# Softmax attention on one core: where a key tile's value matmuls stand in TensorE's order

## The chip, the core and the metric

One NeuronCore of a Trainium2 chip runs the whole program. Five engines work side by side, each through its own queue in order: TensorE (PE, whose weight loads are shown apart as PEld), VectorE (DVE), ScalarE (ACT), GpSimd (POOL) and SyncE (SP, which here only issues DMAs). They meet through semaphores. The metric is the device time of one execution in microseconds (us), the median of the runs. Lower is better.

## The reference, cut to what matters

The model is a chain of six blocks over 2048 tokens of 128 channels. The change touches the softmax attention alone:

```python
qkv = einsum('bsd,ed->bse', x, qkv_w) + qkv_b      # 16 heads of 8 channels
scores = einsum('bhqe,bhke->bhqk', q, k) / sqrt(8) # 2048 queries x 2048 keys for each head
attn = softmax(scores, axis=-1)
out = einsum('bhqk,bhke->bhqe', attn, v)
out = einsum('bsd,ed->bse', out, proj_w) + proj_b
```

The softmax needs the maximum of every query's row before it can take an exponential, so the kernel forms all scores twice: a first pass for the maxima, a second one for the exponentials.

## The kernel before

`softmax_attention` cuts the work into 16 **units**: 4 groups of 4 heads (`GROUPS`, `GH`) by 4 chunks of 512 queries (`CHUNKS`). Units are counted from 0. Units 4 to 11 (groups 1 and 2) run in a hardware loop over the group (L1336 for PE), the others are written out.

**First pass** (`first_pass`, L1253 to L1272): 64 matmuls in a unit, numbered i, each 128 queries by 512 keys, go through four PSUM banks, `S1B`. Two successive matmuls, i even and i+1, make a pair in two banks, and DVE reduces a pair to one column of maxima in one instruction (L1382). Only the even matmul of a pair waits, and it waits until the pair before the last one has been reduced (L1264 and L1265, quoted below). After the 32nd reduction DVE combines the maxima in seven short instructions (L1386 to L1403), and SP writes them into extra rows of `q` with four DMAs (L1175), on which the unit's second pass waits (L1307).

**Second pass** (`unit` of PE, L1288): it walks over 16 key tiles, kt = 0 to 15. For each tile and each of the four heads `score(s)` (L1300) makes one matmul of 128 keys by 512 queries into one of three banks, `S2B`, and waits until the exponential that last used the bank is done. ACT takes the exponential of each score, straight out of PSUM into the buffers `xT` and `xn` in turn (L1359). `weigh` (L1274 to L1286) multiplies the four heads' exponentials of one tile with the values `v`. It waits for all four exponentials of its tile, and is 4 matmuls in f32, which the trace shows as 8 short records, side by side on the array. It runs one tile behind: in tile kt, `weigh(kt - 1)`.

**How the two passes are woven.** While the second pass of a unit runs, the first pass of a later one is done in the gaps. `ahead(s)` (L1294) issues the first-pass matmuls of step s+`LEAD`, LEAD being 12, and the count for each step is in a table:

```python
done = [max(0, (k + 1 - HOLE) * STEPS // (STEPS - HOLE)) for k in range(-1, STEPS)]   # L1124
S1_IN = [range(done[k], done[k + 1]) for k in range(STEPS)]                           # L1125
# in first_pass, L1264 and L1265 (the condition cut): for an even i
pe.wait_ge(s1_used, (g * CHUNKS + qc) * PAIRS + (i // 2 - 1))
```

STEPS is 64 and HOLE is 3, so step k has no first-pass matmul for k = 0 to 2, one for most others, and two for k = 23, 43 and 63. Matmul i is that of step i+3 for steps 3 to 22, of step i+2 for steps 24 to 42, and of step i+1 for steps 44 to 62. Tile kt holds the steps k = 4kt+12 to 4kt+15, modulo 64. The last unit, 15, has nothing to do ahead, and unit 14 only in its tiles 0 to 12.

In what follows S0 to S3 are the four scores of a tile, A0 to A3 the first-pass matmuls that `ahead(s)` to `ahead(s + 3)` issue, W its `weigh`, and R a reduction of a pair on DVE (L1382). Before the change PE's order in a tile is S0 S1 A0 S2 A1 S3 A2 W A3 (L1308 to L1325).

Of the kernel before, what the change touches and what calls it, by code (L numbers as in the profile page):

```python
# [933 lines left out]
def softmax_attention(m):  # L934
# [32 lines left out]
    with ExitStack() as stack:  # L967
# [6 lines left out]
        @block.gpsimd  # L974
        def _(pool):
            for c in range(CHUNKS):
                norm.rstds(pool, c)

            step = Chain(pool, pool_steps)
            step(nc.gpsimd.memset(own_row[:, :], 0.0))  # L980
            for i in range(PARTS):
                step(nc.gpsimd.affine_select(out=own_row[:, :], in_=own_row[:, :], compare_op=ALU.not_equal, fill=1.0,
                                             base=-(ROWS + i * GH), pattern=[[-1, GH]], channel_multiplier=1))
            nc.gpsimd.memset(zeros[:, :], 0.0)
            nc.gpsimd.memset(neg_part[:, :, :], 0.0)
# [121 lines left out]
    with ExitStack() as stack:  # L1107
# [143 lines left out]
        @block.tensor  # L1251
        def _(pe):
            def first_pass(g, qc, i):  # L1253

                h, qt, kc = i // (TPC * CHUNKS), i // CHUNKS % TPC, i % CHUNKS

                if i == 0 and qc > 0:
                    pe.wait_ge(q_loaded[qc], DMAS_Q * (g + 1))
                elif i == 0 and not (isinstance(g, int) and g == 0):
                    pe.wait_ge(q_loaded[qc], DMAS_Q * g)  # L1260
                if qc == 0 and i % (TPC * CHUNKS) == 0 and not (isinstance(g, int) and g == 0):
                    pe.wait_ge(k1_loaded[h], DMAS_K * g)

                if i % 2 == 0 and not (isinstance(g, int) and g == 0 and qc == 0 and i < len(S1B)):  # L1264
                    pe.wait_ge(s1_used, (g * CHUNKS + qc) * PAIRS + (i // 2 - 1))  # L1265


                queries = q[0:ROWS, qc, h, :].rearrange("r (p t) -> r t p", t=TPC)[:, qt, :]
                mm = nc.tensor.matmul(m.ps[:, S1B[i % 4], :], queries,  # L1269
                                      k1[:, h, kc * CHUNK:(kc + 1) * CHUNK], start=True, stop=True)  # L1270
                if i % 2 == 1:
                    mm.then_inc(s1_ready, 1)  # L1272

            def weigh(g, qc, kt, first=False):  # L1274

                u = g * CHUNKS + qc
                if qc == 0 and kt % (TILES // 2) == 0:
                    pe.wait_ge(v_loaded[kt // (TILES // 2)], 16 * (g + 1))
                if kt == 0 and not first:
                    pe.wait_ge(out_stored, u)  # L1280
                pe.wait_ge(exped, u * STEPS + (kt + 1) * GH)
                for h in range(GH):
                    last = nc.tensor.matmul(m.ps[32 * h:32 * h + VC, AVB, :], v[:, kt, h, :],  # L1283
                                            ex[kt % P_RING][:, h, :], start=(kt == 0), stop=(kt == TILES - 1),
                                            skip_group_check=True)
                last.then_inc(av_done, 1)  # L1286

            def unit(g, qc, last, first=False):  # L1288

                u = g * CHUNKS + qc  # L1290
                after = [(g, qc + 1), (g, qc + 2)]
                after = [(a, b) if b < CHUNKS else (a + 1, b - CHUNKS) for a, b in after]

                def ahead(s):  # L1294
                    if last and (qc == CHUNKS - 1 or (qc == CHUNKS - 2 and s + LEAD >= STEPS)):
                        return
                    for i in S1_IN[(s + LEAD) % STEPS]:
                        first_pass(*after[(s + LEAD) // STEPS], i)

                def score(s):  # L1300
                    kt, h = s // GH, s % GH
                    if not (first and s < len(S2B)):
                        pe.wait_ge(exped, u * STEPS + (s - S2_SINCE[s] + 1))
                    nc.tensor.matmul(m.ps[:, S2_BANK[s], :], k2[:, h, kt * P:(kt + 1) * P], q[:, qc, h, :],  # L1304
                                     start=True, stop=True).then_inc(s2_ready, 1)

                pe.wait_ge(max_loaded, DMAS_M * (u + 1))  # L1307
                for kt in range(TILES):  # L1308
                    if qc == 0 and kt % (TILES // 2) == 0:
                        pe.wait_ge(k2_loaded[kt // (TILES // 2)], DMAS_K * (g + 1))  # L1310
                    s = kt * GH
                    score(s)
                    score(s + 1)
                    ahead(s)
                    score(s + 2)
                    ahead(s + 1)
                    score(s + 3)
                    ahead(s + 2)
                    if kt >= 1:
                        weigh(g, qc, kt - 1, first)  # L1320
                    elif qc >= 1:
                        weigh(g, qc - 1, TILES - 1)
                    elif not first:
                        weigh(g - 1, CHUNKS - 1, TILES - 1)
                    ahead(s + 3)  # L1325


            nc.tensor.matmul(m.ps[:, AVB, :], zeros[:, 0:P], zeros[:, :], start=True, stop=True)
            for i in range(STEPS):
                first_pass(0, 0, i)  # L1330
            for i in range(S1_IN[LEAD].start):
                first_pass(0, 1, i)
            unit(0, 0, False, True)
            for qc in range(1, CHUNKS):
                unit(0, qc, False)
            with pe.Fori(1, GROUPS - 1) as g:  # L1336
                for qc in range(CHUNKS):
                    unit(g, qc, False)
            for qc in range(CHUNKS):
                unit(GROUPS - 1, qc, True)  # L1340
            weigh(GROUPS - 1, CHUNKS - 1, TILES - 1)
# [72 lines left out]
    with ExitStack() as stack:  # L1414
# [3 lines left out]
        ahead = Prepare(m, stack, m.gateT, True, 5, 7)  # L1418
# [544 lines left out]
```

## Time and profile before

| what | value |
|---|---|
| median of 3 runs | 1883.54 us (1879.14 to 1883.91) |
| span of the profiled execution | 1880.9 us |
| PE busy over the span | 1635.9 us, 87% |
| DVE busy | 1354.7 us, 72% |
| ACT busy | 836.9 us, 44% |
| softmax attention, second pass | 264 to 1036 us of the span |

The profile shows one execution, and its span runs from the first to the last instruction. "Busy" is the time in which an engine executes, matmuls from start to written result, so that PE can look busy while its array waits. The timeline gives start and length of each instruction, or of a row of equal ones (x2, x4), then in brackets how long the engine had been idle and what it waited for. The start of a bf16 matmul of 512 columns to the start of the next one is 0.22 us at full clock, though each has a length of 0.38 us. The waits list says which line waited for which. The granted clock is given as a share of the full 2.4 GHz.

### The profile page before, as it was taken

To read this page: it belongs to the slowest core of one execution; us is meant where nothing else is said; L and a number is where in the kernel's file an instruction comes from. 1 tells how busy PE (TensorE), PEld (TensorE's weight loads), DVE (VectorE), ACT (ScalarE), POOL (GpSimd) and SP (SyncE) were. 2 spreads that over 40 slices of the span, in tenths; PEclk is the share of its full clock that TensorE was granted. 3 is DMA by queue.
4 is the path that set the end of the run, shared out by engine and by line. 5 is a ranking of instruction groups with operands and counts; after the bars stand their busy time and mean duration, and the time that the engine had idled before them with its cause. 6 is when DMAs were issued, how large, how long until landed. Compare 5 with 4: busy or idle time off the path is not lost. (4 is left out here: it accounts for less than half of the span.)

```text
span 1880.9 us, 23731 instructions
## 1 busy us (share of the span) xinstructions
PE 1635.9 (87%) x7285; PEld 683.8 (36%) x7285; DVE 1354.7 (72%) x1951; ACT 836.9 (44%) x1493; POOL 222.4 (12%) x145
## 2 busy tenths in 40 slices
PE   6987589999999999999998798899994356589999
PEld 3433112222222222222221443366661122256665
DVE  5776788888888778888880577666656999745654
ACT  2433427777676666667778253322223000042222
POOL 2222300000000000000000022211101324301110
PEclk8998659999999999999999899899996777799999
DMA  6000400011001100111000000000000000000000
GB/s 168 2 0 1 135 16 8 14 27 40 9 14 28 30 12 7 27 30 24 2 2 2 1 1 0 1 1 0 0 1 0 0 0 1 0 1 6 6 5 7
DMA packets 32021, 29.49 MB, mean 16 GB/s; under 512 B 7788, under 2 KB 27032, under 8 KB 31928
## 3 DMA queue, kind: packets, MB, share of 16 engines
q1 hardware_dynamic: 31928, 28.31, 5.9%
q8 instruction: 52, 0.85, 0.2%
q14 instruction: 41, 0.34, 0.1%
HBM read 22.13 MB, written 4.19 MB: 14 GB/s over the span
## 5 line engine op out<-in xcount | busy, mean ns | idle before, releaser
L1382 DVE TENSOR_REDUCE mx<-ps 128x1 f32<-128x1024 f32 x512 | 605.2, 1220 | 147.5 <-PE ps L1269 143.2
L1269 PE MATMUL ps<-k,q 72*128 72x512 bf16 x1024 | 403.0, 408 | 11.4 <-DVE mx L1382 9.3
L1304 PE MATMUL ps<-q,k 84*128 84x512 bf16 x1024 | 346.8, 384 | 20.7 <-ACT xn L1359 14.5
L1359 ACT ACTIVATE xT<-ps 128x512 f32<-128x512 f32 x512 | 265.1, 603 | 156.7 <-PE ps L1304 156.6
L1359 ACT ACTIVATE xn<-ps 128x512 f32<-128x512 f32 x512 | 266.2, 603 | 107.4 <-PE ps L1304 107.4
L1269 PEld LDWEIGHTS ps<-k,q 72*128 72x128 bf16 x1024 | 110.1, 115 | 331.4 <-DVE mx L1382 185.4
L854 ACT ACTIVATE silu<-ps 128x512 f32<-128x512 f32 x144 | 85.3, 596 | 265.3 <-PE ps L827 261.9
L1304 PEld LDWEIGHTS ps<-q,k 84*128 84x128 bf16 x1024 | 102.3, 102 | 185.6 <-ACT xn L1359 69.6
L889 DVE TENSOR_TENSOR hid<-ps,silu 128x512 f32<-128x512 f32 x144 | 97.8, 690 | 91.2 <-PE ps L831 89.6
L827 PE MATMUL ps<-xT,ew 128*128 (+1 forms) x288 | 151.0, 606 | 6.5 <-PEq L1750 4.8
L817 PEld LDWEIGHTS ps<-ew,hid 128*128 128x128 f32 x1152 | 138.7, 192 | 30.6 <-issue 29.9
L831 PE MATMUL ps<-xT,ew 128*128 (+1 forms) x288 | 149.0, 599 | 0.0
L486 POOL TENSOR_TENSOR rstd<-var,neg_half 128x4 f32<-128x4 f32 x16 | 16.2, 1014 | 1059.8 <-DVE var L386 1059.8
L817 PE MATMUL ps<-ew,hid 128*128 128x128 f32 x1152 | 139.0, 275 | 0.0
L1283 PE MATMUL ps<-xn,v 128*9 128x512 f32 x1024 | 134.7, 598 | 0.0
L1283 PE MATMUL ps<-xT,v 128*9 128x512 f32 x1024 | 134.7, 598 | 0.0
L878 DVE SCALAR_TENSOR_TENSOR X<-ps,cw,X 128x128 f32<-128x128 f32 (+1 forms) x288 | 81.2, 344 | 66.5 <-PE ps L817 64.6
L266 ACT ACTIVATE square_norm<-centred_norm 128x512 f32<-128x512 f32 x8 | 5.0, 629 | 190.3 <-DVE centred_norm L237 190.3
L770 POOL TENSOR_TENSOR acc<-acc,prod 128x512 f32<-128x512 f32 x56 | 71.2, 1271 | 151.3 <-DVE prod L711 151.3
L1680 PE MATMUL ps<-qs,pick 128*128 128x512 f32 x64 | 46.6, 897 | 47.5 <-DVE qs L1656 38.6
L831 PEld LDWEIGHTS ps<-xT,ew 128*128 128x128 f32 x288 | 55.6, 193 | 70.5 <-issue 70.1
L577 PE MATMUL ps<-hid,wT 128*128 128x512 f32 x128 | 68.3, 616 | 11.3 <-DVE prod L711 11.3
(239 smaller groups left out, 1688.9 us busy)
## 6 DMA issues: line engine op xcount, KB each, us to landing
k<-k_parts SPq DMA_DIRECT2D x90, 64.0 KB
q<-q_parts SPq DMA_DIRECT2D x144, 32.0 KB
k<-k_parts SPq DMA_DIRECT2D x108, 32.0 KB
ew<-in_L_ffn_w_dram SPq DMA_DIRECT2D x2, 1024.0 KB
wraw<-in_L_ffn_w_dram SPq DMA_DIRECT2D x3, 512.0 KB, 6.7
q_parts<-part SPq DMA_DIRECT2D x4, 384.0 KB, 5.3
k_parts<-part SPq DMA_DIRECT2D x4, 384.0 KB, 2.6
v<-values SPq DMA_DIRECT2D x8, 144.0 KB, 4.2
```

What stands on the lines that cost most here:

```text
L770: nc.gpsimd.tensor_tensor(acc[:, e % 2, :], acc[:, (e - 1) % 2, :], prod[:, e % 2, :], ALU.add)\
L817: last = nc.tensor.matmul(m.ps[:, YB[e % 2], j * P:(j + 1) * P], hid[:, e % 2, i, j * P:(j + 1) * P], m.ew2[:, e, i, :], start=(i == 0), s ...
L827: nc.tensor.matmul(m.ps[:, AB[i], :], m.ew1[:, e, i * P:(i + 1) * P], x_c, start=True, stop=True)\
L831: nc.tensor.matmul(m.ps[:, BB[i], :], m.ew3[:, e, i * P:(i + 1) * P], x_c, start=True, stop=True)\
L854: nc.scalar.activation(silu[:, i, :], m.ps[:, AB[i], :], ACT.Silu).then_inc(silu_done, 1)
L878: last = nc.vector.scalar_tensor_tensor(out=x_t[:, j, :], in0=m.ps[:, YB[e % 2], j * P:(j + 1) * P], scalar=cw[:, j, e:e + 1], in1=x_t[:, ...
L889: nc.vector.tensor_tensor(hid[:, e % 2, i, :], m.ps[:, BB[i], :], silu[:, i, :], ALU.mult)\
L1269: mm = nc.tensor.matmul(m.ps[:, S1B[i % 4], :], queries, k1[:, h, kc * CHUNK:(kc + 1) * CHUNK], start=True, stop=True)
L1283: last = nc.tensor.matmul(m.ps[32 * h:32 * h + VC, AVB, :], v[:, kt, h, :], ex[kt % P_RING][:, h, :], start=(kt == 0), stop=(kt == TILES - 1),
L1304: nc.tensor.matmul(m.ps[:, S2_BANK[s], :], k2[:, h, kt * P:(kt + 1) * P], q[:, qc, h, :], start=True, stop=True).then_inc(s2_ready, 1)
L1359: nc.scalar.activation(ex[kt % P_RING][:, h, :], m.ps[:, S2_BANK[s], :], ACT.Exp).then_inc(exped, 1)
L1382: nc.vector.reduce_max(mx[:, h, qt, kc:kc + 1], m.ps[:, 2 * (i % 2):2 * (i % 2) + 2, :], AX.XY)\
```

## The change

In each key tile PE's order becomes S0 S1 W S2 A0 S3 A1 A2 A3. The instructions, their number and their waits stay as they were, as do the orders of the other engines.

```diff
                     s = kt * GH
                     score(s)
                     score(s + 1)
-                    ahead(s)
-                    score(s + 2)
-                    ahead(s + 1)
-                    score(s + 3)
-                    ahead(s + 2)
                     if kt >= 1:
                         weigh(g, qc, kt - 1, first)
                     elif qc >= 1:
                         weigh(g, qc - 1, TILES - 1)
                     elif not first:
                         weigh(g - 1, CHUNKS - 1, TILES - 1)
+                    score(s + 2)
+                    ahead(s)
+                    score(s + 3)
+                    ahead(s + 1)
+                    ahead(s + 2)
                     ahead(s + 3)
```

## Rows read from the trace of the kernel before

**Rows 1.** Busy time by engine, second pass: PE, PEld, DVE, ACT, POOL, clock, DMA.

```profile
262.00:1036.00 774.00, 748.96 (x4027) 208.24 (x4026) 589.59 (x584) 538.97 (x1039) 0.00 (x0) 0.99 0.08 17
```

**Rows 2.** Waits, second pass: who waited for whom, us in total, times, longest.

```profile
PEld ps L1269 <- DVE mx L1382: 148.0, 227, 1.7
```

**Rows 3.** Timeline, tile 11 of a written-out unit: start us, us, engine, line, operation.

```profile
887.22 0.60 PE L1304 MATMUL ps<-q,k 84*128 84x512 bf16 x2
887.64 2.06 ACT L1359 ACTIVATE xn<-ps 128x512 f32<-128x512 f32 x4 [0.77 <-PE ps L1304]
887.65 0.38 PE L1269 MATMUL ps<-k,q 72*128 72x512 bf16 x1
888.07 2.36 DVE L1382 TENSOR_REDUCE mx<-ps 128x1 f32<-128x1024 f32 x2 [0.48 <-PE ps L1269]
...
888.53 0.38 PE L1269 MATMUL ps<-k,q 72*128 72x512 bf16 x1
888.84 1.04 PE L1283 MATMUL ps<-xT,v 128*9 128x512 f32 x8
889.82 0.41 PE L1269 MATMUL ps<-k,q 72*128 72x512 bf16 x1
890.06 0.60 PE L1304 MATMUL ps<-q,k 84*128 84x512 bf16 x2
```

**Rows 4.** Timeline, from A3 of tile 5 to A3 of tile 6, a looped unit.

```profile
725.53 0.41 PE L1269 MATMUL ps<-k,q 72*128 72x512 bf16 x1
...
725.97 2.36 DVE L1382 TENSOR_REDUCE mx<-ps 128x1 f32<-128x1024 f32 x2 [0.69 <-PE ps L1269]
...
727.25 0.41 PE L1269 MATMUL ps<-k,q 72*128 72x512 bf16 x1
727.59 1.05 PE L1283 MATMUL ps<-xn,v 128*9 128x512 f32 x8
728.57 0.41 PE L1269 MATMUL ps<-k,q 72*128 72x512 bf16 x1
```

**Rows 5.** Timeline, W sixteen tiles apart: first looped, then written out.

```profile
518.00 1.05 PE L1283 MATMUL ps<-xT,v 128*9 128x512 f32 x8
...
566.74 1.05 PE L1283 MATMUL ps<-xT,v 128*9 128x512 f32 x8
...
870.75 1.05 PE L1283 MATMUL ps<-xT,v 128*9 128x512 f32 x8
...
918.52 1.04 PE L1283 MATMUL ps<-xT,v 128*9 128x512 f32 x8
```

**Rows 6.** Timeline, S0 of two successive tiles of the last unit.

```profile
1018.48 0.82 PE L1304 MATMUL ps<-q,k 84*128 84x512 bf16 x3
...
1020.86 0.82 PE L1304 MATMUL ps<-q,k 84*128 84x512 bf16 x3
```

**Rows 7.** Timeline, first and last short DVE instruction, then S0 of the next unit.

```profile
748.91 0.19 DVE L1386 TENSOR_REDUCE neg<-mx 128x16 f32<-128x32 f32 x1
...
750.38 0.46 DVE L1403 STREAM_TRANSPOSE neg_turned<-neg_part 128x128 bf16<-128x128 bf16 x1
...
756.80 0.60 PE L1304 MATMUL ps<-q,k 84*128 84x512 bf16 x2 [0.19 <-DMA q<-neg_turned]
```

**Rows 8.** Timeline, the loop's jump back, and the tile after it.

```profile
656.30 1.03 PE L1304 MATMUL ps<-q,k 84*128 84x512 bf16 x2 [2.83 <-issue]
...
657.13 0.63 PE L1269 MATMUL ps<-k,q 72*128 72x512 bf16 x1
...
657.80 1.22 DVE L1382 TENSOR_REDUCE mx<-ps 128x1 f32<-128x1024 f32 x1 [4.38 <-PE ps L1269]
...
659.40 1.90 PE L1283 MATMUL ps<-xn,v 128*9 128x512 f32 x8
...
661.23 0.61 PE L1269 MATMUL ps<-k,q 72*128 72x512 bf16 x1
```

**Rows 9.** Busy time by engine, last unit, columns as in the first group.

```profile
1012.00:1034.00 22.00, 19.25 (x109) 3.83 (x108) 0.00 (x0) 19.21 (x38) 0.00 (x0) 1.00 0.00 1
```

## The prediction

> **What bounds the kernel now.** I first read the busy time of the stage that the change touches, the second pass. PE is busy for 749 of 774 us, DVE for 590, ACT for 539, at a clock of 0.99 [rows 1]. The DMA share is 0.08, so transfers matter only where something waits for one. PE looks full, but a busy PE says little, so I went to the waits: its first-pass matmuls waited 148.0 us, in 227 places, for a reduction on DVE [rows 2]. Part of that is only a weight load with nothing to do while W's matmuls run, and costs nothing. The timeline decides, and two kinds of tile are to be told apart there.
>
> In tile 11 of a unit, S0 starts at 887.22 and the next tile's S0 at 890.06: 2.84 us [rows 3]. Its pieces are S0 to S1 0.22, S1 to A0 0.21, A2 to W 0.31, W to A3 0.98, A3 to S0 0.24, and 0.22 for the rest. PE never stands still here, it is the bound. The reduction row belongs to the pair that A0 completes: it starts 0.42 after A0. Two reductions take 2.36 and then DVE idles 0.48 in each tile.
>
> In tile 6 it is different: from A3 to A3 3.04 us [rows 4]. A3 completes a pair, its reduction starts 0.44 later, A2 of the next tile starts 1.28 after that, W 0.34 later and A3 0.98 later, and 0.44 + 1.28 + 0.34 + 0.98 = 3.04. That is a closed loop through DVE: A2 begins a new pair, and the pair's banks are those of the pair before the last one, which has to be reduced first. So the reduction, with its 1.22 us and the way there and back, 1.70 in all, already sets the pace where a pair is completed behind W and needed again before the next W.
>
> Which tile is of which kind follows from the table of steps. In steps 3 to 22 and 44 to 62 the even matmul falls on an odd step: pairs are (A1, A2) and (A3, next A0). Those are tiles 14, 15, 0, 1, 2 and 8 to 12; I call them **split** tiles, since a pair is split over two tiles. In steps 24 to 42, tiles 3 to 7, pairs are (A0, A1) and (A2, A3): **whole** tiles.
>
> **The change part by part.** No instruction is added or removed. W moves from behind A2 to behind S1, A0 moves behind S2, A1 and A2 behind S3.
>
> *PE's own time.* The switch into W and out of it are there once, as before. I take 0.31 from S1 to W, 0.98 from W to S2, 0.24 from S2 to A0 (the first matmul after W also has 0.24 behind it now, A3 to S0), and 0.22 for each of the other steps [rows 3]. A tile without a wait is then 0.22 + 0.31 + 0.98 + 0.24 + 5 x 0.22 = 2.85, I take the 2.84 measured. Bounds for the moved switches are -0.05 and +0.05 a tile, the spread between 0.31 and 0.34 and between 0.22 and 0.24 in [rows 3, 4]; zero is nearest, since the same kinds of matmul meet.
>
> *Waits for exponentials.* With S0 at 0, W would start at 0.53, S2 at 1.51, A0 1.75, S3 1.97, A1 2.19, A2 2.41, A3 2.62, next S0 2.84. ACT starts 0.42 after a score [rows 3] and does four in 2.06, a pitch of 0.49 and a last one of 0.60. S3's exponential then runs from 2.42 to 3.02, and W of the next tile, at 3.37, has it with 0.3 to spare. S3 needs S0's bank, free at 1.1. So W's earlier place costs nothing in the usual tile; the cover is the three first-pass matmuls between S3 and the next S0. Where they are missing it costs: tile 13 has only A3, lasts 2.19, and W in tile 14 waits until 0.88 instead of 0.53, 0.35 more.
>
> *Waits for reductions, whole tiles.* A1 is at 2.19, its reduction runs from 2.61, that of (A2, A3) follows about 1.2 behind, from 3.80, and frees A2 at 5.08. A2 of the next tile comes at 2.84 + 2.41 = 5.25. The loop of 3.04 is gone, and PE is the bound again: 2.84, a gain of 0.20 a tile. What is late next is the same loop, with 0.17 to spare.
>
> *Waits for reductions, split tiles.* This is the large term. A3 begins a pair and needs the reduction of the pair that A0 of its own tile completed. Before, A0 and A3 stood 2.17 apart [rows 3], and 0.42 + 1.28 = 1.70 fitted in, with 0.47 over. Now A0 stands behind W, and A0 to A3 is 0.87. A3 has to wait 0.83, and S0, S1 and W of the next tile are queued behind it on PE. The loop from A0 to A0 is 0.42 (to the reduction) + 1.28 (to A3) + 0.24 (S0) + 0.22 (S1) + 0.31 (W) + 0.98 (S2) + 0.24 (A0) = 3.69, in place of 2.84. DVE has its 2.36 us of reductions in the tile as before, and idles 1.3 us of it, since the pair it could start next waits for A0 behind W.
>
> *A unit, summed.* Tiles 3 to 6: 4 x 2.84 = 11.36. Tile 7 is whole, but its A3 step has two matmuls, i = 41 and 42. The second begins a pair and needs (A0, A1) reduced: 2.19 + 0.42 + 1.28 = 3.89, and S0 0.24 later, 4.13. Tiles 8 to 11: 4 x 3.69 = 14.76. Tile 12 has a double step too, 3.91. Tile 13: 2.19. Tile 14: 3.69 + 0.35 = 4.04. Tiles 15, 0, 1: 11.07. Tile 2, double: 3.91. Together 55.37. Before, a unit took 48.74 in the loop and 47.77 written out [rows 5]. So +6.6 for each of the 8 looped units and +7.6 for units 1, 2, 3, 12 and 13.
>
> *The maxima's DMA.* In tile 12 the last three reductions now run one after another behind A3: the last ends 2.3 after A3, DVE's seven short instructions, 1.93 in all, take it to 4.3, and S0 of the next unit came 5.96 after the last of them ended [rows 7], so it can start 10.2 after A3. By the sum above it is due at 0.46 + 2.19 + 4.04 + 3.69 = 10.4. No wait is left, by a margin of 0.2; if the margin is wrong by 0.3 it costs 0.1 to 0.3 a unit, 4 us at most.
>
> *The ends.* Unit 0 starts without W and at half clock, where PE rather than DVE is the bound: I take off 1.5, so 6.1. Unit 14 has first-pass work in tiles 0 to 12: new 45.4, before 39.0 (47.77 less 8.8, three tiles of 2.84 and an estimate of 0.3 for a wait at the unit's end), +6.4. In unit 15 there is none, and before a tile took 2.38 [rows 6]. With W behind S1 the loop is W to S2 0.98, to its exponential 0.42, that and the next one 0.49 + 0.60, back to W 0.05: 2.54, so 0.16 x 15 = 2.4, and 0.6 for the later maxima: +3.0. The tile behind the loop's jump runs at half clock, as below, where the stall is small: -1.5.
>
> Sum: 8 x 6.6 + 5 x 7.6 + 6.1 + 6.4 + 3.0 - 1.5 = **104.8 us**. The blocks behind are untouched. The span goes from 1880.9 to 1985.7. The median of the runs is 2.6 above that span, so I forecast 1883.5 + 104.8 = 1988.3, rounded to 1988.
>
> **The rivals.**
>
> *The clock falls.* In a stalled tile PE stands idle for 0.83 of 3.69 us. In the trace, after 2.83 us of idleness at the loop's jump, PE ran at half clock, 1.2 GHz: W to A3 takes 1.83 there instead of 0.98 [rows 8]. Against it: in the last unit a tile takes 2.38 [rows 6] and its pieces 3 x 0.22 + 0.31 + 0.98 = 1.95, so that PE stands idle for 0.43, 18% against 22% here, and the clock stays at 1.00, that is 2.4 GHz [rows 9]. There a matmul takes 0.42 (S0 to A0 is two of them), A0 to its reduction 0.67, and A2 to W 0.59 (what four matmuls from A0 leave up to W), so the same loop is 0.67 + 1.28 + 0.42 + 0.42 + 0.59 + 1.83 + 0.42 = 5.63 [rows 8]. The slow stretch reaches over the 4.9 us of those rows at least; I take 6, in which a stalled kernel falls behind by 6 x (1 - 3.69/5.63) = 2.1 us. With one in each of a unit's two runs of split tiles, 4.2 us for 14 units, 59 us: 2047. The Trainium skill (TensorE: Matmul & The Clock Gate, "A second HAM failure mode: psum-queue depth-cycling") tells of a bf16 kernel that cycled through PSUM banks and idled so often between groups that its clock swung between the two levels. By that rule the time is this rival's; the trace of before, with its own short idle times in most tiles at a clock of 0.99 [rows 1], speaks against it as far as it goes.
>
> *Faster, because the reduction doesn't bite.* If A3 in split tiles found its banks free, all tiles would take 2.84: the whole tiles gain 0.20 (4 of them, and about 0.4 in tile 7), and the looped units would lose the 0.97 by which they are longer than the others [rows 5], 0.55 a unit on average. That is 1.75 a unit, for 14 units 25 us: 1859. The point of decision is whether A0 to A3 is longer than 1.70. It is 0.87 by every pitch of the trace, and the same loop can be seen closing in whole tiles [rows 4]. It would take a pairing of matmuls other than the one I derived; the reduction that follows A0 by 0.42 in tile 11 [rows 3] speaks against that.
>
> *Slower by less.* If the stalled stretches slip so that only one of the two runs of split tiles is held up, or whatever PE saves elsewhere is larger, the sum is about half: 1935. I see no mechanism in the trace for it; it stands for an error in the count of tiles.
>
> **How the numbers follow.** Forecast: 0.71. Clock: 0.15. Half: 0.06. Faster: 0.06. That the order on the chip changes nothing at all: 0.02; PE runs its queue in order, and the moved W is in it. The sum's own bounds are 0.05 a tile over some 220 tiles, 11 us, 4 for the DMA, and 8 for the ends. This makes 1965 to 2011 around the forecast. The range is to reach the clock rival too: 1965 to 2055, which leaves out the two smaller cases and some of the clock's. A measurement of this kernel can tell 0.3%, 5.7 us, from no change. Faster 0.06, same 0.03, slower 0.91.
>
> **What would show it.** In the changed kernel's timeline: A0 to its reduction 0.42, the reduction to A3 1.28, and an idle PE before A3 in split tiles, with DVE named as the releaser; tile to tile 3.69 in tiles 8 to 11, 2.84 in tiles 3 to 6; DVE idle for over 1.2 us in each split tile; and W without any wait for ACT save in tile 14. The span from 264 to 1036 would become some 877 us. In unit 15 a tile would take 2.54. A granted clock under 0.95 in the stage would speak for the clock rival. The prediction is wrong if split tiles show no wait at A3, or if W waits for exponentials in every tile.

## The result and the profile after

The changed kernel takes 1990.72 us (median of 4 runs, 1985.26 to 1996.43) against 1883.72 for the kernel before. The ratio is 1.0576, 95% interval 1.0548 to 1.0604: 5.8% slower, 107.0 us. The forecast was 1988 and +104.8.

The profiled execution has a span of 1983.5 us, 102.6 more than the one of before. The first score of the second pass starts at 264.2 before and at 262.0 after, the last one at 1034.3 and at 1135.8. So the second pass went from 770.1 to 873.8 us, +103.7. The rest differs by little: 2.2 less ahead of it and 1.1 more behind it, in stretches whose code is the same. The 2.2 lie ahead of the first first-pass matmul, which starts at 218.7 before, at 216.5 after, and between 216.5 and 221.5 over all the profiles of this case.

The busy time by engine in that stage, with the columns of [rows 1]:

```profile
262.00:1139.00 877.00, 750.83 (x4023) 208.53 (x4023) 584.05 (x582) 560.56 (x1040) 0.00 (x0) 0.99 0.07 15
```

PE is busy for 2 us more than before and DVE for 6 less, in 103 us more. ACT is busy for 22 us more, though it has the same exponentials: four in one row took 2.06 us [rows 3], and now they come as two rows of two, 1.09 each, with idle time between. Nothing was added; the engines wait. The clock is 0.99 as in [rows 1]. The waits of the stage, and below them, for PE's matmuls, the same line of before:

```profile
DVE mx L1382 <- PE ps L1269: 239.4, 223, 7.1
PEld ps L1269 <- DVE mx L1382: 187.9, 162, 1.4
...
PE ps L1269 <- DVE mx L1382: 110.6, 162, 0.9
...
PEld ps L1304 <- DMA q<-neg_turned: 1.9, 1, 1.9
```

```profile
PE ps L1269 <- DVE mx L1382: 3.5, 15, 0.2
```

The third line is the change: PE's own matmuls, not only their weight loads, now wait 110.6 us for reductions, in 162 places, against 3.5 us in 15 places before. The second line answers to [rows 2] and has grown from 148.0 to 187.9, which alone would not say much. DVE waits for PE 239 us at the same time (131 before): each waits for the other in turn. The line on the DMA says that the maxima's DMA held up one unit, which is the last one, at 1095.40.

The timeline of a looped unit shows both kinds of tile side by side, from A0 of tile 7 (whole, with two matmuls at A3) to S0 of the tile behind the first split one:

```profile
790.09 0.38 PE L1269 MATMUL ps<-k,q 72*128 72x512 bf16 x1
...
790.53 0.81 PE L1269 MATMUL ps<-k,q 72*128 72x512 bf16 x3
790.95 2.36 DVE L1382 TENSOR_REDUCE mx<-ps 128x1 f32<-128x1024 f32 x2 [0.47 <-PE ps L1269]
792.23 0.41 PE L1269 MATMUL ps<-k,q 72*128 72x512 bf16 x1 [0.89 <-DVE mx L1382]
792.48 0.60 PE L1304 MATMUL ps<-q,k 84*128 84x512 bf16 x2
...
793.00 1.05 PE L1283 MATMUL ps<-xn,v 128*9 128x512 f32 x8
793.98 0.39 PE L1304 MATMUL ps<-q,k 84*128 84x512 bf16 x1
794.21 0.38 PE L1269 MATMUL ps<-k,q 72*128 72x512 bf16 x1
...
794.62 2.36 DVE L1382 TENSOR_REDUCE mx<-ps 128x1 f32<-128x1024 f32 x2 [1.32 <-PE ps L1269]
794.64 0.60 PE L1269 MATMUL ps<-k,q 72*128 72x512 bf16 x2
795.91 0.41 PE L1269 MATMUL ps<-k,q 72*128 72x512 bf16 x1 [0.67 <-DVE mx L1382]
796.15 0.60 PE L1304 MATMUL ps<-q,k 84*128 84x512 bf16 x2
796.68 1.04 PE L1283 MATMUL ps<-xT,v 128*9 128x512 f32 x8
```

In the split tile A0 is at 794.21, its reduction starts at 794.62 (0.41 later, against 0.42 in [rows 3]), A3 at 795.91 (1.29 after that, 1.28 in [rows 4]) and next W at 796.68. W to W is 3.68. DVE stood still for 1.32, mostly while W ran. PE stood still for 0.67 by the profile; A3 starts 0.83 later than the pitch of 0.22 behind A2 would give, since a matmul's row (0.38) is longer than the pitch. A whole unit, by W in tile 3 and sixteen tiles on:

```profile
780.43 1.04 PE L1283 MATMUL ps<-xn,v 128*9 128x512 f32 x8
783.25 1.05 PE L1283 MATMUL ps<-xT,v 128*9 128x512 f32 x8
...
788.88 1.05 PE L1283 MATMUL ps<-xT,v 128*9 128x512 f32 x8
793.00 1.05 PE L1283 MATMUL ps<-xn,v 128*9 128x512 f32 x8
...
811.61 1.04 PE L1283 MATMUL ps<-xT,v 128*9 128x512 f32 x8
814.15 1.05 PE L1283 MATMUL ps<-xn,v 128*9 128x512 f32 x8
...
835.56 1.05 PE L1283 MATMUL ps<-xn,v 128*9 128x512 f32 x8
```

Whole tiles 2.82, tile 7 4.12, split tiles 3.68, from W of tile 13, which has only one first-pass matmul, to W of tile 14, which waits for exponentials, 2.54 (811.61 to 814.15), a unit 55.13 where it was 48.74 and 47.77 [rows 5].

### The profile page after: what moved, and what is told of

The parts are those of the page before. It is cut to its first block and busy times, and to the rows that moved or that the text cites. A ratio compares the mean times of both kernels' runs of the same rounds, so it can differ in the third digit from the quotient of the medians.

```text
span 1983.5 us, 23710 instructions
## 1 busy us (share of the span) xinstructions
PE 1638.8 (83%) x7272; PEld 684.9 (35%) x7285; DVE 1351.0 (68%) x1951; ACT 857.9 (43%) x1493; POOL 222.4 (11%) x145
## 5 line engine op out<-in xcount | busy, mean ns | idle before, releaser
L1269 PE MATMUL ps<-k,q 72*128 72x512 bf16 x1024 | 352.0, 403 | 132.6 <-DVE mx L1382 116.3
L1359 ACT ACTIVATE xT<-ps 128x512 f32<-128x512 f32 x512 | 278.2, 596 | 193.7 <-PE ps L1304 193.5
L1359 ACT ACTIVATE xn<-ps 128x512 f32<-128x512 f32 x512 | 278.1, 595 | 159.0 <-PE ps L1304 158.4
L1304 PEld LDWEIGHTS ps<-q,k 84*128 84x128 bf16 x1024 | 97.9, 99 | 307.0 <-ACT xn L1359 122.3
L889 DVE TENSOR_TENSOR hid<-ps,silu 128x512 f32<-128x512 f32 x144 | 97.8, 689 | 90.4 <-PE ps L831 88.8
L1680 PE MATMUL ps<-qs,pick 128*128 128x512 f32 x64 | 45.5, 876 | 47.1 <-DVE qs L1656 39.7
```

What stands on the lines that cost most here:

```text
L889: nc.vector.tensor_tensor(hid[:, e % 2, i, :], m.ps[:, BB[i], :], silu[:, i, :], ALU.mult)\
L1269: mm = nc.tensor.matmul(m.ps[:, S1B[i % 4], :], queries, k1[:, h, kc * CHUNK:(kc + 1) * CHUNK], start=True, stop=True)
L1359: nc.scalar.activation(ex[kt % P_RING][:, h, :], m.ps[:, S2_BANK[s], :], ACT.Exp).then_inc(exped, 1)
```

## The experiments

Two theories were to be told apart. **Reduction**: PE waits at the start of a pair for the reduction of the pair before the last, because W now stands between the two matmuls that close that loop. **Exponentials**: W comes too early behind the scores of the tile before, and PE and ACT wait for each other. The ratio of each run is to the kernel before, measured beside it (1883.0 to 1883.9 us). The edits are against the changed kernel unless said otherwise.

**A0 back in front of W.** The order is S0 S1 A0 W S2 A1 S3 A2 A3; W stays early.

```diff
                     score(s + 1)
+                    ahead(s)
                     if kt >= 1:
                         weigh(g, qc, kt - 1, first)
...
                     score(s + 2)
-                    ahead(s)
-                    score(s + 3)
                     ahead(s + 1)
+                    score(s + 3)
                     ahead(s + 2)
```

> Order S0 S1 A0 W S2 A1 S3 A2 A3: W stays early, only A0 goes back in front of it. Theory 'reduction' (in split tiles A3 waits for the reduction of the pair that A0 completes, 1.70 us from A0 to A3, and W between A0 and A3 hides it): the wait before A3 goes, split and whole tiles both take 2.82 to 2.85 us, a unit falls from 55.1 to about 46.4, plus 0.8 to 1.8 where the maxima's DMA now ends last at a unit's start, the kernel from 1991 to 1877 (1865 to 1890). Rival 'exponentials' (W comes too early for the exponentials of the tile before, and PE and ACT wait for each other): W is as early as in the changed kernel, so tiles stay near 3.7 us and the kernel at 1985 to 1995.

Measured: 1914.25 us, ratio 1.0170 (1.0139 to 1.0200). Moving one matmul takes back 76 of the 107 us with W where the change put it, which "exponentials" excludes. But it is 37 more than expected. Split tiles are at 2.82 as forecast; whole tiles are at 3.24:

```profile
886.45 0.38 PE L1269 MATMUL ps<-k,q 72*128 72x512 bf16 x1
...
886.86 2.36 DVE L1382 TENSOR_REDUCE mx<-ps 128x1 f32<-128x1024 f32 x2 [0.89 <-PE ps L1269]
...
888.15 0.41 PE L1269 MATMUL ps<-k,q 72*128 72x512 bf16 x1 [0.23 <-DVE mx L1382]
888.48 1.05 PE L1283 MATMUL ps<-xT,v 128*9 128x512 f32 x8
889.46 0.39 PE L1304 MATMUL ps<-q,k 84*128 84x512 bf16 x1
889.69 0.38 PE L1269 MATMUL ps<-k,q 72*128 72x512 bf16 x1
```

Here A1 (886.45) completes a pair and A0 of the next tile (888.15) needs it reduced, with W behind that A0 and A1 behind W: 0.41 + 1.29 + 0.33 + 0.98 + 0.23 = 3.24. I had followed the loop in split tiles only, and the same theory gives this one. It is 0.42 in each of tiles 3 to 6, 1.7 a unit. A unit takes 49.84 (W at 882.00 and at 931.84), and the rest of the miss lies in two places. Tiles 2 and 7, with two matmuls at A3, take 3.68 and 3.89, where their own matmuls need 3.04. At the unit's end, in tile 14 (3.67), A3 waits behind DVE's seven short instructions, which the later last pair has pushed back.

**A0 directly behind W**, one place earlier than in the change: S0 S1 W A0 S2 A1 S3 A2 A3.

```diff
-                    score(s + 2)
                     ahead(s)
-                    score(s + 3)
+                    score(s + 2)
                     ahead(s + 1)
+                    score(s + 3)
                     ahead(s + 2)
```

> Order S0 S1 W A0 S2 A1 S3 A2 A3: A0 stays behind W, only one matmul nearer to it. Theory 'reduction': the closed loop of a split tile loses one step of 0.22 to 0.24 us, from 3.68 to 3.45, and tile 7 the same; whole tiles stay at 2.82. A unit falls by 11 x 0.23 to 52.6, the kernel by 35 to 1955 (1948 to 1963). Rival 'exponentials': one place among the first-pass matmuls changes nothing, 1985 to 1995.

Measured: 1959.29 us, 1.0392 (1.0366 to 1.0419), inside the range forecast for "reduction" and 31 under the changed kernel. A0, its reduction, A3, W and the next A0 in a split tile:

```profile
884.78 0.41 PE L1269 MATMUL ps<-k,q 72*128 72x512 bf16 x1
...
885.23 2.36 DVE L1382 TENSOR_REDUCE mx<-ps 128x1 f32<-128x1024 f32 x2 [1.12 <-PE ps L1269]
...
886.51 0.41 PE L1269 MATMUL ps<-k,q 72*128 72x512 bf16 x1 [0.45 <-DVE mx L1382]
...
887.28 1.05 PE L1283 MATMUL ps<-xT,v 128*9 128x512 f32 x8
888.26 0.41 PE L1269 MATMUL ps<-k,q 72*128 72x512 bf16 x1
```

0.45 + 1.28 + 0.77 + 0.98 = 3.48, where 3.45 was expected. The step that was taken out of the loop, S2, is what the tile lost.

**Half of each reduction.** Half of the keys are left out of the maxima.

```diff
-                    nc.vector.reduce_max(mx[...], m.ps[:, 2 * (i % 2):2 * (i % 2) + 2, :], AX.XY)\
+                    nc.vector.reduce_max(mx[...], m.ps[:, 2 * (i % 2):2 * (i % 2) + 2, 0:CHUNK // 2], AX.XY)\
```

> The changed kernel, but each reduction of a pair reads only half of the columns of its two banks, so that half of the keys are left out of the maxima. By a line through the reductions of 32 and of 1024 elements (0.19 and 1.22 us) it takes 0.69 instead of 1.22. Theory 'reduction': a split tile's loop falls by 0.53, from 3.68 to 3.15, a unit by 11 x 0.53 to 49.3, the kernel by some 78 to 1912 (1900 to 1925), since a wait for the maxima's DMA may come up. Rival 'exponentials': PE and ACT do what they did, 1985 to 1995. Whole tiles stay at 2.82 by both.

Measured: 1894.51 us, 1.0050 (1.0034 to 1.0067). PE's and ACT's work is the same and 96 of the 107 us are gone, more than the 78 expected. The tiles are as forecast:

```profile
844.21 0.38 PE L1269 MATMUL ps<-k,q 72*128 72x512 bf16 x1
...
844.63 1.34 DVE L1382 TENSOR_REDUCE mx<-ps 128x1 f32<-128x512 f32 x2 [1.80 <-PE ps L1269]
...
847.35 0.38 PE L1269 MATMUL ps<-k,q 72*128 72x512 bf16 x1
```

A0 to A0 is 3.14 (3.15 expected), and the units take 49.26. The second pass runs from 257.9 to 1048.3, 83.4 less than in the changed kernel. The rest is ahead of it: the first pass of unit 0 has 32 reductions with no other work, and from its first matmul to the first score it takes 36.7 instead of 45.5. I had left these 8.8 us out of the sum. The profiled execution shows only 4.1 of them, because there this first pass began 4.7 later (221.2 against 216.5). The DMA wait that I allowed for did not come. The medians say 96 where the two spans differ by 88.8; the runs of the changed kernel spread over 11 us.

**Only whole pairs**, in the order of the change. The table has no first-pass matmul in steps 0 to 3, one in each later step and two more in steps 23 and 43.

```diff
-LEAD = 12
+LEAD = 16
...
-        done = [max(0, (k + 1 - HOLE) * STEPS // (STEPS - HOLE)) for k in range(-1, STEPS)]
+        done = [max(0, k - 4) + 2 * (k > 23) + 2 * (k > 43) for k in range(STEPS + 1)]
```

> The changed kernel's order, with another table of steps: no first-pass matmul in steps 0 to 3, one in each later step, and two more in each of steps 23 and 43, so that every pair is (A0, A1) or (A2, A3); LEAD is 16 for 12, so that the maxima's DMA has a tile more. Theory 'reduction': there are no split tiles, all take 2.82 but the two with three matmuls at A3, which wait for (A0, A1) and take about 4.35. A unit is about 47.9 in place of 55.1, the kernel 1890 (1878 to 1905). Rival 'exponentials': W's place is the same and the pairing does not matter to ACT, 1985 to 1995.

Measured: 1888.45 us, 1.0028 (1.0013 to 1.0042); 1890 was expected. The order is exactly the change's, and 102 of its 107 us are gone with the split pairs. A0 to A0 over a tile:

```profile
734.25 0.38 PE L1269 MATMUL ps<-k,q 72*128 72x512 bf16 x1
...
735.11 2.36 DVE L1382 TENSOR_REDUCE mx<-ps 128x1 f32<-128x1024 f32 x2 [0.46 <-PE ps L1269]
...
737.07 0.38 PE L1269 MATMUL ps<-k,q 72*128 72x512 bf16 x1
```

2.82, no wait on PE. Against the kernel before, the change's order gains nothing even with whole pairs alone. The tiles with three matmuls at A3 take 4.33 (4.35 expected), a unit 48.19 in the loop (47.9 expected).

**LEAD 16 alone**, with the old table, to share out that gain.

```diff
-LEAD = 12
+LEAD = 16
```

> The changed kernel with LEAD 16 for 12 and its old table, so with split tiles: it tells whether LEAD or the table made the gain of the run with whole pairs. Theory 'reduction': a tile's kind depends on the pairing alone, 3.68 and 2.82 as before, 55.1 a unit, the kernel at 1991 (1984 to 1998). Rival 'lead' (more time between the maxima and their unit is what was missing): 1885 to 1920.

Measured: 1985.75 us, 1.0539 (1.0517 to 1.0560). Units take 55.13 as with LEAD 12. So the pairing made the gain, not the distance to the unit.

**No hole**: one first-pass matmul in every step, all pairs whole, in the order of the change.

```diff
-LEAD = 12
+LEAD = 16
...
-HOLE = 3
+HOLE = 0
```

> The changed kernel's order with LEAD 16 and HOLE 0: one first-pass matmul in each of the 64 steps, so all pairs are whole and no A3 step has more than one. Theory 'reduction': all tiles 2.82 (45.1 a unit); DVE's seven short instructions, 1.93 us, now meet first-pass work, of which some 0.8 us reaches PE, since a tile leaves DVE 0.46 of slack to catch up. A unit 46.0 (45.6 to 46.6) against 48.1 with whole pairs and a hole, the kernel 30 less than that one's 1888: 1858 (1850 to 1868). Rival 'hole': without the hole PE waits for all of the 1.93 us and more in each unit, 47.1 or over, 1874 or more.

Measured: 1880.77 us, 0.9982 (0.9964 to 1.0000). The rival "hole" was right here: a unit takes 47.13 instead of 46.0. Thirteen tiles are at 2.82, but one takes 4.58, 1.76 more: DVE makes its short instructions, and then two pairs in a row find their banks not yet reduced, where I had counted the first alone. In three of the 16 units it got worse:

```profile
452.46 4.62 DVE L1382 TENSOR_REDUCE mx<-ps 128x1 f32<-128x1024 f32 x4 [0.42 <-DVE neg_turned L1403]
...
453.74 0.41 PE L1269 MATMUL ps<-k,q 72*128 72x512 bf16 x1 [1.09 <-DVE mx L1382]
...
454.87 0.63 PE L1269 MATMUL ps<-k,q 72*128 72x512 bf16 x2 [0.29 <-DVE mx L1382]
...
456.28 1.90 PE L1283 MATMUL ps<-xn,v 128*9 128x512 f32 x8
```

After 1.09 us of idleness in one piece and 0.29 more, W has the length of half clock (1.90, as in [rows 8]), and such a unit takes 1.6 longer. It is the clock rival, in a kernel that I had not suspected of it. But the waits alone don't bring it: an earlier unit of the same execution has the same two, 1.09 and 0.29, and its W is at full clock:

```profile
359.49 0.41 PE L1269 MATMUL ps<-k,q 72*128 72x512 bf16 x1 [1.09 <-DVE mx L1382]
...
361.61 1.04 PE L1283 MATMUL ps<-xn,v 128*9 128x512 f32 x8
```

The longer units and the three falls, 14 x 1.1 and 3 x 1.6, are 20 of the 23 us by which the forecast missed.

**The order of before, with the same table**, LEAD being 14 where it was 16. The edit is to the kernel before.

```diff
-LEAD = 12
+LEAD = 14
...
-HOLE = 3
+HOLE = 0
```

> The kernel before, order S0 S1 A0 S2 A1 S3 A2 W A3, with LEAD 14 and HOLE 0, so that all its pairs are whole. Theory 'reduction': with W between A2 and A3 every tile closes the loop of 3.04, 48.6 a unit and some tenths for DVE's short instructions, against 48.3 before: 1890 (1883 to 1900). So neither the order nor the table alone gains. Rival 'table' (HOLE 0 alone is what helps): 1855 to 1865.

Measured: 1947.10 us, 1.0320 (1.0281 to 1.0359). Tiles close the loop of 3.04 throughout, as expected; here by W, one tile, and then the tile that meets DVE's short instructions:

```profile
458.01 1.05 PE L1283 MATMUL ps<-xn,v 128*9 128x512 f32 x8
461.05 1.04 PE L1283 MATMUL ps<-xT,v 128*9 128x512 f32 x8
...
470.24 1.04 PE L1283 MATMUL ps<-xn,v 128*9 128x512 f32 x8
474.92 1.04 PE L1283 MATMUL ps<-xT,v 128*9 128x512 f32 x8
```

The time is 57 over the forecast, and two things show: that tile takes 4.68, 1.6 more than the others, and the granted clock over the stage is 0.94:

```profile
262.00:1100.00 838.00, 801.93 (x4024) 221.33 (x4026) 590.24 (x584) 540.39 (x1039) 0.00 (x0) 0.94 0.07 16
```

The units without a fall of the clock take 50.65 to 50.87, the others 52.2 to 57.3. So neither the order nor the table gains by itself, and both together, at 0.9982, are level with the kernel before.

**The last unit in the old order**, S0 S1 S2 S3 W, where no first-pass matmuls are left. It was tried three times, with these tables: LEAD 14 and no hole; LEAD 16 and no hole; LEAD 16 and two steps of hole. So the first differs from the run without a hole in LEAD as well.

```diff
+                    late = last and qc == CHUNKS - 1
                     score(s)
                     score(s + 1)
+                    if late:
+                        score(s + 2)
+                        score(s + 3)
...
-                    score(s + 2)
-                    ahead(s)
-                    score(s + 3)
-                    ahead(s + 1)
-                    ahead(s + 2)
-                    ahead(s + 3)
+                    if not late:
+                        score(s + 2)
+                        ahead(s)
+                        score(s + 3)
+                        ahead(s + 1)
+                        ahead(s + 2)
+                        ahead(s + 3)
...
# the third of them has LEAD = 16 and this table
+        done = [max(0, k - 2) + 2 * (k > 35) for k in range(STEPS + 1)]
```

> As the run with HOLE 0, but LEAD 14 for 16, and in the last unit, which has no first-pass matmuls, the order S0 S1 S2 S3 W of the kernel before. Theory 'reduction' with 'exponentials' where no first-pass matmul covers them: the last unit's tiles go from 2.54 back to 2.38, 16 x 0.16 = 2.6 less, and 1 to 2 less at the start, where fewer first-pass matmuls stand ahead of the first score: 1854 (1846 to 1864), 1.5% under the kernel before. If the unit's maxima now come late, up to 1 a unit is lost and it is 1868.

> As the run with LEAD 16 and HOLE 0, and only the last unit in the order S0 S1 S2 S3 W. Where no first-pass matmul stands between S3 and the next W, W behind S1 waits for exponentials: 2.54 a tile, against 2.38 with W behind S3. So 16 x 0.16 = 2.6 less than that run's 1880.8: 1878 (1870 to 1885), 0.3% under the kernel before. If W's place costs nothing even there, 1881.

> The same last unit and LEAD 16, but first-pass matmuls from step 2 on and two extra ones in step 35: whole pairs, no first-pass matmul while DVE makes its seven short instructions. Theory 'reduction': the tile behind the hole waits 0.5 instead of 1.8, the tile with three at A3 takes 4.33, 12 or 13 others 2.82: 47.1 a unit, the same as with HOLE 0, 1878 (1868 to 1890). Against it: if the extra pair's wait of 1.5 us makes the clock fall, some 2 us for each time, 1885 to 1900.

Measured, in this order: 1885.60 us, 1.0004 (0.9982 to 1.0026); 1873.36, 0.9947 (0.9933 to 0.9960); 1873.00, 0.9945 (0.9931 to 0.9958). The last unit does what was expected. First two tiles of the changed kernel there, by W, then two of the second run:

```profile
1114.23 1.05 PE L1283 MATMUL ps<-xT,v 128*9 128x512 f32 x8
1116.77 1.05 PE L1283 MATMUL ps<-xn,v 128*9 128x512 f32 x8
```

```profile
1005.81 1.05 PE L1283 MATMUL ps<-xT,v 128*9 128x512 f32 x8
1008.19 1.05 PE L1283 MATMUL ps<-xn,v 128*9 128x512 f32 x8
```

2.54 against 2.38: that is the cost that the rival "exponentials" speaks of, and it shows only where no first-pass matmuls cover it, here and behind tile 13. The first run missed its 1854 by 32 us, 23 of which are the miss of the run without a hole, from whose forecast it was derived. With LEAD 14 the maxima come out in the middle of a tile; the long tile grew from 4.58 to 5.12, and the clock fell more often (0.97 over the stage).

The second run has 7.4 us less than the same kernel without the late order, where 2.6 were expected. Their profiles are 7.9 apart. The last unit, from its first W to its last, takes 34.6 instead of 38.2, 3.5 less: 0.16 a tile in most, and the last two W stand 0.86 apart instead of 2.54. The other 4.0 are a first pass that starts at 217.1 instead of 221.1, ahead of anything that the edit touches, so they are no gain of the order.

The third, whose waits are split over two places, came out at the same time, 5 under my 1878 and well under the 1885 to 1900 of a falling clock. Its tile with three matmuls at A3 takes 4.33, 1.1 more than its 10 matmuls and W need (2.82 + 2 x 0.22), and the one behind the hole 3.72, 0.9 more than 2.82, where 0.5 was expected; with these the clock stayed at 0.99. Both are 0.5% under the kernel before, and the intervals leave out 1. In the profiles the stretch from the first first-pass matmul to the last score is 12.4 and 11.0 us shorter than before.

## Why the prediction was right

Point by point, against its own steps:

- *What bounds.* That PE stands at its bound in split tiles and at the loop of 3.04 in whole ones held. In the changed kernel whole tiles went to 2.82 (2.84 forecast), so the gain is there: 0.22 in each of four tiles.
- *Split tiles.* The large term. 3.69 forecast, 3.68 measured, with DVE idle 1.32 (1.3) and the releaser at A3 as named. Its causes were changed one by one: the place of A0 (-31 us for one place, -76 for its return before W), the length of the reduction (-96 for half of it, of which some 9 lie in the first pass of unit 0), and the pairing (-102, together with LEAD, which alone left a unit at 55.13).
- *The unit's sum.* 55.37 forecast, 55.13 measured; tile 7 4.13 and 4.12. Looped and written-out units now take the same: the small extra of the looped ones, 0.97 a unit before, has vanished, as the sum had it, without my knowing what it was. The traces show where it stood: before, most split tiles of a looped unit take 2.91 instead of 2.84 and one takes some 0.3 more, while the whole tiles are at 3.04 in both kinds of unit. Its cause stays open. Part of the sum's closeness is luck. The units grew by 0.2 less than summed, 7.4 and 6.4, and the 1.5 us taken off for the tile behind the loop's jump did not come: that unit grew by 6.6. In the looped units the two cancel, 51.3 forecast and 51.4 measured.
- *The ends and the DMA.* 2.54 a tile in the last unit, forecast and measured. The margin of 0.2 us for the maxima's DMA held; apart from the very first score PE waits for it once, ahead of the last unit, 1.39 us where it was 0.59 before. That is 0.8 for the later maxima, where the sum has 0.6.
- *The total.* +104.8 forecast; +103.7 by the stage, +102.6 by the spans, +107.0 by the medians, where the 95% interval of the ratio, 0.0056 wide, is some 11 us. What of the last digits is luck can't be said.
- *The clock rival.* 0.99 in the stage, so it did not happen. That the kernel stayed clear of it was less safe than its 0.15 suggested: without a hole, where the profile shows idle times of 1.09 and 0.29 us and here 0.67, it fell in three units. The prediction also called the idle times of before those of most tiles; by W to W only 7 of a written-out unit's 16 tiles last longer than 2.84. The Trainium skill (TensorE: Matmul & The Clock Gate, "A second HAM failure mode: psum-queue depth-cycling") has the frequent idling between groups of matmuls as what makes the clock swing. The trace of the changed kernel does not agree with that: it idles in 11 of 16 tiles and keeps 0.99. The runs without a hole, which idle in fewer places, have such falls.
- *What the forecast lacked.* It followed the loop for the two orders at hand. The first experiment showed that it holds for whole pairs as well when A0 stands before W, and missing that is part of the 37 us by which the expectation was off.

## What to carry to other kernels

When an instruction of an in-order engine is moved, find every pair of places between which another engine has to return a buffer, and add up what now stands on the way, once round; the moved block need not touch that buffer at all. Here a 1 us block of value matmuls, put between the matmul that completes a pair and the one that needs the pair's turn of the banks, made a loop of 3.68 us out of one that had 0.47 us to spare. And a rotation has a phase: with two instructions to a buffer and an irregular table the same order can be the best in one tile and the worst in the next, so check the parity of each before judging an order by a single tile.

## What the runs showed of the hardware

Short idle times of PE are not alike for its clock. In the changed kernel PE waits in 11 of a unit's 16 tiles, by 0.67 us in the profile's rows (0.89 in tile 7), and the granted clock stays at 0.99 over 877 us. Without a hole it waits in one place of a unit, 1.09 and then 0.29 us, and in the profiled execution the clock fell to 1.2 GHz behind that wait in three units but not in the others, which have the same wait: W took 1.90 us instead of 1.04, and the unit 1.6 us more. With the order of before and no hole the clock was 0.94 over the stage, and units took up to 5.4 us more than the undisturbed 50.9, and 6.5 more where the loop's jump came on top. With waits of 1.1 and 0.9 us in two tiles far apart (the last run above) it was 0.99 over 763 us. What decides it these runs don't tell.
